# Own blocks of keys scored in two products by the sign of the decay, 14 signed key blocks and a ring of three quads, in an attention kernel on one core

## The reference, cut to what matters

```python
scores = jnp.einsum('bhqd,bhkd->bhqk', qh, kh) * scale
decay = jnp.exp(-LAMBDA_DECAY * TIME_STEP * jnp.abs(idx[:, None] - idx[None, :]))
scores = scores * decay[None, None, :, :]
attn = jax.nn.softmax(scores, axis=-1)
out = jnp.einsum('bhqk,bhkd->bhqd', attn, vh)
```

## Time and profile before

| | us |
|---|---|
| median of 3 runs | 536.9 (535.86 to 537.37) |
| the profiled execution | 537.57 |
| its span, first to last instruction | 535.8 |
| PE busy | 492.9 (92%) |
| ACT busy | 490.4 (92%) |
| DVE busy | 277.0 (52%) |
| POOL busy | 218.1 (41%) |

### The profile page before, as it was taken

The page is one execution under the profiler, slowest core; times in us unless marked ns, Lnnn a source line. Parts: engine busy times, 40 slices in busy tenths (PEclk is TensorE's granted clock), DMA queues, the critical chain, the costliest instruction groups (busy, mean ns, idle before and its releaser), DMA issues.

```text
span 535.8 us, 9389 instructions
## 1 busy us (share of the span) xinstructions
PE 492.9 (92%) x3457; PEld 114.0 (21%) x3457; DVE 277.0 (52%) x641; ACT 490.4 (92%) x534; POOL 218.1 (41%) x281
## 2 busy tenths in 40 slices
PE   8868999999999999999999999999999999999971
PEld 3311211221121211221121212222111212121220
DVE  5513454454744555554754554554555645455546
ACT  3756999999999999999999999999999999999951
POOL 0889306974251218993251217994101211002110
PEclk9997999999999999999999999999999999999985
DMA  6478879746997100757977000757987000100000
GB/s 174 122 253 209 256 232 235 262 149 211 256 201 180 49 5 29 278 171 217 256 166 178 9 5 7 272 170 223 260 183 164 22 7 7 47 0 1 1 21 24
DMA packets 49108, 73.79 MB, mean 138 GB/s; under 512 B 6113, under 2 KB 26529, under 8 KB 49057
## 3 DMA queue, kind: packets, MB, share of 16 engines
q1 hardware_dynamic: 48240, 72.85, 49.3%
q10 hardware_dynamic: 816, 0.28, 0.2%
HBM read 35.40 MB, written 35.65 MB: 133 GB/s over the span
## 4 chain that ended last, share of the span: by engine, by line
PE 44%; ACT 32%; issue 9%; DVE 5%; POOL 4%; DMA 3%; SPq 2%; DVEq 0%; POOLq 0%; ACTq 0%
ACT probs L749 32%; PE ps L948 23%; PE ps L932 13%; PE ps L850 1%; PE ps L845 1%; PE ps L813 1%; DVE ps L1173 1%; DMA qp_dram<-parts 1%; PE ps L822 1%; PE ps L817 1%; DMA Qs<-qp_dram 1%; POOL sq L575 1%; DMA X<-L_attn_x 1%; SPq L442 1%; POOL sq L587 1%
## 5 line engine op out<-in xcount | busy, mean ns | idle before, releaser
L749 ACT ACTIVATE probs<-ps 128x1024 f32<-128x1024 f32 x512 | 479.7, 1070 | 18.7 <-DVE ps L1173 12.9
L948 PE MATMUL ps<-probs,V 128*9 128x512 f32 x2048 | 269.5, 598 | 3.9 <-DVE pv_out L1181 1.2
L1173 DVE TENSOR_TENSOR ps<-ps,consts 128x256 f32<-128x256 f32 (+1 forms) x256 | 144.1, 565 | 184.5 <-PE ps L932 177.6
L932 PE MATMUL ps<-Qs,Ks 64*128 64x512 bf16 x992 | 182.0, 387 | 18.4 <-ACT probs L749 5.4
L932 PEld LDWEIGHTS ps<-Qs,Ks 64*128 64x128 bf16 x992 | 43.8, 93 | 290.4 <-ACT probs L749 269.6
L948 PEld LDWEIGHTS ps<-probs,V 128*9 128x9 f32 x2048 | 31.4, 88 | 79.9 <-issue 60.5
L636 POOL TENSOR_TENSOR xs<-xs,magic 128x512 f32<-128x512 f32 x7 | 8.9, 1277 | 93.7 <-DVE magic L1234 93.7
L553 POOL TENSOR_SCALAR rs<-mv 128x4 f32<-128x4 f32 (+1 forms) x10 | 2.3, 228 | 82.7 <-DVEq L1355 82.0
L575 POOL TENSOR_TENSOR sq<-kT,decay 128x256 f32<-128x256 f32 (+2 forms) x13 | 16.3, 1250 | 48.1 <-DVE kT L1273 34.4
L1181 DVE COPY pv_out<-ps 105x512 f32<-105x512 f32 x31 | 21.4, 691 | 25.6 <-PE ps L948 25.6
L587 POOL TENSOR_TENSOR sq<-sq,parts 128x1024 f32<-128x1024 f32 (+1 forms) x16 | 29.4, 1835 | 1.3
(11 more groups left out here) (148 smaller groups left out, 282.2 us busy)
## 6 DMA issues: line engine op xcount, KB each, us to landing
Qs<-qp_dram SPq DMA_DIRECT2D x26, 512.0 KB, 9.5
qp_dram<-parts SPq DMA_DIRECT2D x16, 768.0 KB, 4.9
Ks<-kp_dram SPq DMA_DIRECT2D x26, 384.0 KB, 5.8
kp_dram<-parts SPq DMA_DIRECT2D x12, 384.0 KB, 3.8
kp_dram<-parts SPq DMA_DIRECT2D x6, 768.0 KB, 4.8
qp_dram<-parts SPq DMA_DIRECT2D x8, 512.0 KB, 6.1
Qs<-qp_dram SPq DMA_DIRECT2D x12, 256.0 KB, 8.4
X<-L_attn_x SPq DMA_DIRECT2D x10, 256.0 KB, 3.3
```

The costliest lines, as they stand in the source:

```text
L749: nc.scalar.activation(probs[:, quad % RING, 2 * jp:2 * jp + 2, :].rearrange("p j n -> p (j n)"), ps_all[:, bank * CH:(bank + 2) * CH], AC ...
L932: last = nc.tensor.matmul(bank, Ks[half, g, jp, key_cols(v, kc)], Qs[half, g, jp, qh, v, :], start=True, stop=True)
L948: last = nc.tensor.matmul(pv[32 * j:32 * j + VW, :], V[:, unit // 2 * NB + kc, HG * j + g, :], probs[:, quad % RING, j, :], start=i == 0, ...
L1173: nc.vector.tensor_tensor(own, own, factors, ALU.mult).then_inc(fixed, 1)
```

## The change

Own blocks after the first group are scored in two products: the columns on the MINUS side with the MINUS operands, those on the PLUS side with the PLUS ones, so that only the diagonal's 128 columns are fixed for every r. For r = 1 each of a slot's two matmuls of 512 columns becomes 256 + 256 columns, for r = 2 it becomes 384 + 128; r = 0 and r = 3 keep one. Both signs of more blocks are needed: 14 blocks (KN = 1792), 10 early and 4 late. The parts of the early keys are 1280 columns instead of 1024 (batch 0: 768, then 512), multiplied as 384 + 896 instead of 256 + 768. To hold them, `parts` is two tensors, `rest` covers both halves of `sq`, and the ring of `probs` shrinks to three quads.

```diff
-KP = S - 2 * P
-KN = 2 * KP
+KE = 3 * P
+KN = KL + KE + S - P
...
-    at = KP + (kc - 2) * P if v == 1 else KL + kc * P if kc < 2 else (kc - 2) * P
+    at = KL + KE + (kc - 1) * P if v == 1 else KL + kc * P if kc < 3 else (kc - 3) * P
...
-RING = 4
+RING = 3
...
 def variant(quad):
...
-    if r < 2:
-        return PLUS, (0, (r + 1) * P, (1 - r) * P)
-    return MINUS, (r * P, CH, 2 * P)
+    if quad < F32_GROUPS * NB:
+        return (PLUS, (0, (r + 1) * P, (1 - r) * P)) if r < 2 else (MINUS, (r * P, CH, 2 * P))
+    return (PLUS, (0, P, P)) if r == 0 else (MINUS, (r * P, (r + 1) * P, 2 * P))
+
+
+def spans_of(quad):
+
+    v, own = variant(quad)
+    if own is None or own[1] == CH or v == PLUS:
+        return [(v, slice(0, CH))]
+    return [(MINUS, slice(0, own[1])), (PLUS, slice(own[1], CH))]
...
-        parts = sb("parts", [P, 2, PARTS, S], BF16)
+        parts = sb("k_parts", [P, PARTS, KN - KL], BF16), sb("q_parts", [P, PARTS, S], BF16)
         sq = sb("sq", [P, 2, S])
-        rest = sq[:, 0, :]
+        rest = sq[:, :, :].rearrange("p a n -> p (a n)")
...
-            early_keys = (slice(KL, 2 * KL), slice(2 * KL, KN))
+            early_keys = (slice(KL, KL + 6 * P), slice(KL + 6 * P, KN))
...
-                decayed_keys(PLUS, slice(0, 2 * P), 0)
-                decayed_keys(MINUS, slice(2 * P, S), 2 * P)
-                split(0, S, 0)
+                decayed_keys(PLUS, slice(0, KE), 0)
+                decayed_keys(MINUS, slice(P, S), KE)
+                split(0, KN - KL, 0)
...
-            decayed_keys(PLUS, slice(0, 2 * P), 0)
-            decayed_keys(MINUS, slice(2 * P, CH), 2 * P)
-            split(0, CH, 0)
+            decayed_keys(PLUS, slice(0, KE), 0)
+            decayed_keys(MINUS, slice(P, CH), KE)
+            split(0, 6 * P, 0)
...
-                        last = nc.tensor.matmul(bank, Ks[half, g, jp, key_cols(v, kc)],
-                                                Qs[half, g, jp, qh, v, :], start=True, stop=True)
+                if quad >= F32_GROUPS * NB:
+
+                    for v, cols in spans_of(quad):
+                        for i in range(2):
+                            half = slice(64 * i, 64 * i + 64)
+                            last = nc.tensor.matmul(ps[:, 2 * (s % 3) + i, cols], Ks[half, g, jp, key_cols(v, kc)],
+                                                    Qs[half, g, jp, qh, v, cols], start=True, stop=True)
```

More of the change, by code:

```diff
@@ L387, in store_keys @@
                     rows = slice(PARTS * j, min(PARTS * j + PARTS, PRODUCTS))
-                    sp.dma_start(kp_dram[b, :, rows, to], parts[:, 0, j:j + 1, at:at + n]
+                    sp.dma_start(kp_dram[b, :, rows, to], parts[0][:, j:j + 1, at:at + n]
                                  .broadcast_to([P, rows.stop - rows.start, n])).then_inc(parts_out[0], 16)
@@ L395, in store_queries @@
                     sp.dma_start(qp_dram[b, :, rows, qh * S:(qh + 1) * S],
-                                 parts[:, 1, 0:rows.stop - rows.start, :]).then_inc(parts_out[1], 16)
+                                 parts[1][:, 0:rows.stop - rows.start, :]).then_inc(parts_out[1], 16)
             def load_keys(b, g, cols, count):
@@ L457, in _ @@
             load_queries(0, 1, slice(0, 1), stage_in[1])
-            store_keys(0, "early keys 1", early_keys[1], KL)
+            store_keys(0, "early keys 1", early_keys[1], 6 * P)
             sp.wait_ge(parts_out[0], 16 * STORED * 2)
@@ L579, in decayed_queries @@
                 q2 = qT[:, cols].rearrange("p (o n) -> p o n", o=1).broadcast_to([P, 2, CH])
-                chain(nc.gpsimd.tensor_tensor(rest.rearrange("p (v n) -> p v n", v=2), q2, decay[:, :, cols], ALU.mult))
+                chain(nc.gpsimd.tensor_tensor(rest[:, 0:S].rearrange("p (v n) -> p v n", v=2), q2, decay[:, :, cols],
+                                              ALU.mult))
             def split(which, n, at):
                 r = rest[:, 0:n]
-                to = [parts[:, which, k, at:at + n] for k in range(PARTS)]
+                to = [parts[which][:, k, at:at + n] for k in range(PARTS)]
                 chain(nc.gpsimd.tensor_copy(to[0], r))
@@ L592, in split_queries_of_first_group @@
             def split_queries_of_first_group():
-                r, q = rest, Q0.rearrange("p v n -> p (v n)")
-                to = [parts[:, 1, k, :] for k in range(PARTS)]
+                r, q = rest[:, 0:S], Q0.rearrange("p v n -> p (v n)")
+                to = [parts[1][:, k, :] for k in range(PARTS)]
                 chain(nc.gpsimd.tensor_copy(to[0], q))
@@ L620, in late_keys @@
                 stored_before(b, 0, 1)
-                decayed_keys(PLUS, slice(2 * P, KP), 0)
+                decayed_keys(PLUS, slice(KE, KE + KL), 0)
                 split(0, KL, 0)
@@ L663, in _ @@
             decayed_keys(MINUS, slice(CH, S), 0)
-            split(0, CH, CH)
+            split(0, CH, 6 * P)
             late_keys(0)
@@ L929, in qk @@
                                                 start=True, stop=True)
-                    else:
-                        half = slice(64 * i, 64 * i + 64)
-                        last = nc.tensor.matmul(bank, Ks[half, g, jp, key_cols(v, kc)],
-                                                Qs[half, g, jp, qh, v, :], start=True, stop=True)
+                if quad >= F32_GROUPS * NB:
[4 more added lines that the diff above has]
+                                                    Qs[half, g, jp, qh, v, cols], start=True, stop=True)
                 last.then_inc(qk_done, 1)
```

## The result

The changed kernel takes 545.55 us (median of 6 runs, 544.09 to 547.38), beside 537.13 for the kernel before (6 runs, 535.86 to 540.03, the three shown above among them). The ratio is 1.0138, with a 95% interval of 1.0112 to 1.0163: slower by 7.4 us (6.0 to 8.8). Its profiled execution took 544.82, with a span of 543.0, 7.2 us over that of before.

What follows compares the result with a forecast made beforehand. It took ACT's exps and PE's attention matmuls as the bound, with fixes 1% of the chain. Costs 2.6 + 3.2 + 1.0 + 1.7 + 0.6 + 0.6 less 2.5 gave +7.2 on 537.57, adjusted by 0.7: 544.1 us, range 537.0 to 550.0.

Steps and rivals of the forecast that it cites:

- Start: Before group 1: POOL's longer first split and a load larger by 128 KB cost +2.6 us (2.0 to 3.2).
- Unit 1: Gather of group 3: POOL's later keys (2.06) and the larger store ahead (1.1) cost +3.2 us (2.1 to 4.4).
- Unit 2: Gather behind three larger stages of loads, POOL's delay already paid by then: +1.7 us (0 to 2.5).
- Units 3 and 5: Same order as unit 1 with more time: gather 0.8 late, some hidden, +0.5 us each (0 to 4.0 for both).
- Units 4 and 6: Gather behind larger loads with 2.3 us of slack: +0.3 us each (0 to 3.8 together), POOL's 2.06 possibly on top.
- the landing: Units 4 and 6: the gather's last transfer, issued at 280.31, would land at 282.3, before DVE at 284.56.
- Pieces and ring: PE's 248 added matmuls from split products cost 0.6 us (0 to 4); the probs ring of three costs 0.
- the rule of the Trainium skill: About 60 cycles overhead per matmul: 6.2 us of PE in place of 1.2, the sum some 2 us higher.
- Gain: Narrow fixes give 2.5 us (0.6 to 7): 1.3 by chain share, 1.2 for group 1's first blocks and isolated late slots.
- Signs: Expected profile readings: group 1's scores near 43, recip waits some 3 us in units 1 and 2, DVE busy 33 less.

Runs made afterwards that it cites:

- e8: e7 with the two blocks only narrow fixes need split with the second early keys, and group 1's fixes left wide: 537.37 us, ratio 0.9988.
- e5: Kernel before with a ring of three and POOL splitting 256 more key columns that nobody stores or reads: 542.44 us, ratio 1.0063.
- e4: Changed kernel with one product for each block, narrow fixes kept (some signs wrong): 546.15 us, ratio 1.0158.
- e1: Changed kernel with the wide fixes and single products of before, still splitting, storing and loading 14 blocks: 546.68 us, ratio 1.0172.
- e6: Changed kernel with the gather of group 3 ahead of the loads for the next batch's group 2, in second units: 544.21 us, ratio 1.0101.
- e3: Kernel before with only the fixes narrowed to the diagonal's 128 columns from group 1 on (some signs wrong): 538.29 us, ratio 1.0001.
- e2: Changed kernel with the next batch's early keys stored behind the gather of group 3 instead of ahead of it: 552.8 us, ratio 1.0285.
- e9: Kernel before with both new SP orders, those of e2 and e6: 538.06 us, ratio 1.0006.
- e7: Changed kernel with the edits of e2 and e6 together: 537.87 us, ratio 0.9983.
- e10: e8 with all fixes wide and all products single, everything else the same: 537.3 us, ratio 0.9999.

## Why the prediction was right

The time came out at 545.55, 1.4 above the forecast of 544.1, within the range, and for the reasons given: the new costs on POOL and in the DMA queue reach the exps through the gathers, and the narrow fixes give back little. By its steps, with the profile's values:

- **Start:** +2.6 foretold, +2.5 found, and e8 gives all of it back (the scatter of such starts is up to 1.6).
- **Unit 1:** +3.2 foretold, +3.1 found. POOL's 2.06 stands against 2.2 in e5, the queue's 1.1 against 0.9. That the queue's part came out so near is luck in part: it was set between two bounds, and e4 lost 4.8 at this place. POOL's new pieces took what they were costed at: 2.63 us for a subtraction of 1280 columns, 2.10 for the multiplication of 896.
- **Behind unit 1:** nothing foretold, +1.0 found, the lower clock after PE's idle time. This step was missing. In e1 it was 2.5, in e5 1.5; the same stall is not always charged the same.
- **Unit 2:** +1.7 foretold, 0.0 found. The step failed where it said that POOL's delay "is paid by then" and counted the growth of the loads on top: the gather did land 4.7 us later (DVE starts at 168.99 instead of 164.33), but PE was 5.2 us later itself, the clock's 1.0 included. An earlier stall pays for a later one; I read this from the two times, and no run tests it alone.
- **Units 3 and 5:** 0.5 each foretold. Each lost 1.0 at quad 8 and won 0.4 back by quad 12, so 0.6 each stayed. But only about half of the 1.0 is the late gather that I had reckoned with: in unit 3 DVE goes on at 231.26 instead of 225.49, 0.65 more than exps were late by then. The other half is widen_sums, which took 1.26 us instead of 0.74 (last section), and that was in no step.
- **Units 4 and 6:** 0.3 each foretold. Unit 4 lost 1.4 and won 0.4 back, unit 6 lost 0.1. The step that failed is the landing. I took 1.96 us for it, from a gather behind a store, and it took 6.9 behind loads (e6). POOL's 2.06, of which I wrote that it comes on top, was not in it: the last transfer was issued no later than exps were late.
- **Pieces and ring:** 0.6 and 0 foretold. e4 finds nothing for the pieces and e5 nothing for the ring. As for the rule of the Trainium skill (TensorEngine Tiling, Instruction Overhead), no run here shows 60 cycles for each matmul: PE is busy for 0.7 us more for 248 more of them, not for the 6.2 of the estimate by that rule.
- **Gain:** 2.5 foretold. e3 shows 0.8 after group 1 and 0.5 in it, 1.3 together. That is what the chain's share gave; the 1.2 that I added for idle exps at wide fixes were wrong. Of group 1's -1.42 in the changed kernel only 0.5 is theirs. The rest is the clock: the group began 2.5 us later while its clock came back at nearly the same time (46.6 us into the span instead of 46.2), so less of it ran at 1.2 GHz. Pairs of kernels in which the clock came back equally long after the group's first exp show both parts. Against the kernel before and by quad 12, after 2.1 us e2 (narrow) won 1.60 and e9 (wide) 1.07; after 2.8 and 2.9 us e7 (narrow) won 1.31 and e10 (wide) 0.76; after 4.6 us e6 (narrow) won 0.52, where the kernel before (wide) has 0 by definition.
- **Signs:** group 1's first scores start at 42.84, the recip of unit 1 waits 3.22 us, and 26.1 us are lost after slot 21 instead of 20.2. Two signs failed: the recip of unit 2 waits 0.69 us and not some 3, and DVE's busy time fell by 29.6 us and not 33, since seven widen_sums took 1.4 us longer in all, and seven of another instruction as much.

So the mechanism is shown, but that the sum came out within 0.2 us of the change by the profiles (7.2 in both) is luck. Unit 2 (1.7) and the pieces (0.6) were put in and not found; the clock behind unit 1 (1.0) was left out, the gain was taken too high by 1.2, and units 3 to 6 kept some 0.5 more than foretold; and the clock gave 0.9 back in group 1, which no step had. These nearly cancelled.

## What to carry to other kernels

Read how much of the chain an instruction holds before making it cheaper: these fixes were 27% of the span in DVE's busy time and 1% of the chain, and taking 33 us off them gave 1.3 by the steps and nothing that the times can tell. Then follow what pays for it, here more operands, through every queue written in a fixed order: small urgent transfers behind a store or a load are slowed by its bytes. And when one order is put right, look for the buffer or queue that is next; e2's single line cost some 8 us (by the ratios) until the second order took the loads out of the way.

## What the runs showed of the hardware that I had not expected

**DVE and POOL get in each other's way.** widen_sums (L1206) reads two SBUF tensors and writes one of 128x512. It takes 0.69 us alone. In unit 3 of the changed kernel it met one of POOL's multiplications. DVE's line, then POOL's:

```profile
231.85 1.26 DVE L1206 TENSOR_TENSOR wide<-rec,consts 128x512 f32<-128x512 f32 x1
...
231.29 1.27 POOL L585 TENSOR_TENSOR sq<-kT,decay 128x512 f32<-128x512 f32 x1
232.62 0.95 POOL L597 CAST k_parts<-sq 128x512 bf16<-128x512 f32 x1
```

POOL's ran its usual 1.27 us and ended at 232.56; DVE's took 0.57 longer than alone and ended 0.55 after it. Then POOL's cast took 0.95 instead of 0.61. So most of DVE's work seems to have been done after POOL's end. This adds 0.4 to 0.6 us to the path at units 1, 3 and 5, and is a part of what those units lost (unit 1: 1.10 us). It fits the Trainium skill (GPSIMD Engine Reference, Specifications), which says that GpSimd's SBUF interfaces are shared with VectorE, with contention for instructions with two SBUF inputs. With POOL idle the same instruction took 0.69 in units 2, 4, 6 and 7.

**The clock after a stall.** PE's granted clock fell to the lower level after unit 1's stall in each of the five kernels that had it (the changed one, e1, e4, e5, e6), for 3.4 or 6.8 us, and cost 1.0 to 2.5 us. After the stalls of 1.4 us and less it did not fall; in e2 it fell after each stall of 4 us and more. So stalls of 2.2 to 3.2 us at quad 8 cost 3.7 to 5.7 us in all, and e4's of 4.8 cost 6.5. In PE's timeline of the changed kernel the first pair of scores behind the stall takes 0.61 us, and a pair after the clock has come back 0.39:

```profile
111.45 0.61 PE L946 MATMUL ps<-Qs,Ks 64*128 64x512 bf16 x2 [2.82 <-ACT probs L760]
...
116.15 0.39 PE L946 MATMUL ps<-Qs,Ks 64*128 64x512 bf16 x2
```
